# Long cross attention taken by pairs of heads, with 64-row score tiles and key copies of 16 partitions

## The reference

```
q = norm(x) @ Wq          # 128 x 256, 16 heads of 16 features
k = ctx @ Wk              # 12544 x 256
v = ctx @ Wv              # 12544 x 256
for each head h:
    s = q_h @ k_h.T / 4 + mask          # 128 x 12544
    o_h = softmax(s, axis=-1) @ v_h     # 128 x 16
x = x + concat(o) @ Wo
```

## Time and profile before

| | |
|---|---|
| median of 3 runs | 1845.32 us |
| the profiled execution | 1845.17 us |
| its span, first to last instruction | 1843.4 us |
| TensorE matmul busy | 1623.4 us (88%) |
| TensorE weight load busy | 1237.0 us (67%) |
| VectorE busy | 1068.7 us (58%) |
| ScalarE busy | 900.1 us (49%) |
| mean granted TensorE clock | 0.941 |

### The profile page before, as it was taken

One profiled execution on the slowest core, in us unless ns is written; L12 is line 12 of the kernel. 1 busy time (PEld: TensorE's weight loads), 2 busy tenths in 40 slices (PEclk: granted clock), 3 DMA queues, 4 the chain that ended last, 5 costly groups with the idle time before them and its releaser, 6 DMA issues.

```text
span 1843.4 us, 34030 instructions
## 1 busy us (share of the span) xinstructions
PE 1623.4 (88%) x13482; PEld 1237.0 (67%) x13482; DVE 1068.7 (58%) x1958; ACT 900.1 (49%) x1439; POOL 15.1 (1%) x23
## 2 busy tenths in 40 slices
PE   0597997458999999999997797999999999999499
PEld 0365476236787878888785465788878788888356
DVE  6422322447677777777785325777767777777322
ACT  0011031003777777767785120776677676778221
POOL 0000000100000000000000000000000000000000
PEclk9799988669999999999998798999999999999599
DMA  8356754127654555656332175665635446550354
GB/s 351 115 185 198 265 140 128 83 114 157 144 141 101 121 120 125 143 125 151 81 82 81 61 284 121 153 145 124 159 82 141 101 121 139 125 120 2 137 234 179
DMA packets 42811, 257.09 MB, mean 139 GB/s; under 512 B 9929, under 2 KB 10185, under 8 KB 33993
## 3 DMA queue, kind: packets, MB, share of 16 engines
q1 hardware_dynamic: 42664, 255.05, 50.0%
HBM read 152.12 MB, written 0.13 MB: 83 GB/s over the span
## 4 chain that ended last, share of the span: by engine, by line
PE 81%; DMA 7%; DVE 7%; SPq 2%; ACT 2%; issue 2%; POOL 1%; POOLq 0%; DVEq 0%; ACTq 0%
PE T L534 16%; PE O L635 12%; PE S L611 10%; PE S L539 7%; PE O L534 7%; PE T L586 6%; PE T L599 5%; PE O L697 4%; PE O L586 3%; PE O L599 3%; PE S L814 2%; DMA ctx_in<-in_ctx_cols 2%; DMA wide<-in_ctx_rows 2%; PE O L847 2%; DMA wide<-in_up_L0f 2%
## 5 line engine op out<-in xcount | busy, mean ns | idle before, releaser
L1224 DVE CUSTOM_DVE_ANT_0 sc<-S,mask_bias,small 128x896 f32<-128x896 f32 x448 | 513.3, 1146 | 181.6 <-PE S L611 180.5
L926 ACT ACTIVATE sc<-sc,small 128x1792 f32<-128x1792 f32 x224 | 399.6, 1784 | 0.0
L534 PE MATMUL T<-consts,sc 128*128 128x128 f32 (+1 forms) x2200 | 336.3, 277 | 8.8 <-ACT sc L1015 6.4
L534 PEld LDWEIGHTS T<-consts,sc 128*128 128x128 f32 (+1 forms) x2200 | 260.7, 141 | 83.4 <-issue 49.3
L912 ACT ACTIVATE pT<-T 128x512 f32<-128x512 f32 (+1 forms) x446 | 232.0, 523 | 160.3 <-PE T L534 160.3
L611 PE MATMUL S<-keys,q 128*128 128x512 f32 (+1 forms) x896 | 291.8, 407 | 1.4 <-DMA keys<-keys_hl 1.4
L635 PE MATMUL O<-pT,arena 128*32 128x128 f32 x6272 | 238.8, 276 | 0.0
L635 PEld LDWEIGHTS O<-pT,arena 128*32 128x32 f32 x6272 | 179.1, 109 | 37.4 <-issue 37.2
L534 PE MATMUL O<-consts,sc 128*128 128x128 f32 x1048 | 166.7, 276 | 0.0
L912 ACT ACTIVATE pT<-O 128x512 f32<-128x512 f32 (+1 forms) x226 | 118.0, 522 | 84.6 <-PE O L534 84.6
L534 PEld LDWEIGHTS O<-consts,sc 128*128 128x128 f32 x1048 | 125.1, 140 | 35.0 <-issue 24.2
(11 more groups left out here) (281 smaller groups left out, 1453.0 us busy)
## 6 DMA issues: line engine op xcount, KB each, us to landing
keys<-keys_hl SPq DMA_DIRECT2D x448, 224.0 KB, 5.7
ctx_in<-in_ctx_cols SPq DMA_DIRECT2D x42, 896.0 KB, 7.3
wide<-in_up_L3f SPq DMA_DIRECT2D x8, 2048.0 KB, 9.0
wide<-in_ctx_rows SPq DMA_DIRECT2D x14, 896.0 KB, 5.5
wide<-in_up_L0f SPq DMA_DIRECT2D x8, 1408.0 KB, 9.3
sc<-in_ctx_cols SPq DMA_DIRECT2D x10, 896.0 KB, 7.9
wide<-in_up_L2f SPq DMA_DIRECT2D x8, 1024.0 KB, 6.6
wide<-in_down_L2f SPq DMA_DIRECT2D x8, 1024.0 KB, 4.8
```

The lines of the kernel that those rows point to most:

```text
L534: last = nc.tensor.transpose(out[0:w, t * P:(t + 1) * P], src[:, t * w:(t + 1) * w], ident)
L926: nc.scalar.activation(sc[:, n % 3, :], sc[:, n % 3, :], ACT.Exp, bias=n_best[c % 2][:, h:h + 1], scale=-1.0, accum_out=l_new[c % 2][:, h: ...
L1224: V.tensor_tensor_reduce(sc[:, n % 3, i * HC:(i + 1) * HC], S4f[:, i * 2 * BANK:i * 2 * BANK + HC], mask_bias[:, i * HC:(i + 1) * HC], 1.0 ...
```

## The change

The heads are taken in pairs. The order of the contraction's rows changes so that each head has 64 rows of its own: head 0 of a pair rows 0 to 63, head 1 rows 64 to 127, each with four groups of 16. The queries' zeros go. A score step now makes half a chunk for both heads: for each column range one matmul on the upper 64 rows of the array and one on the lower. The turned weights of both heads (28 blocks) go in seven fillings of a bank, and `pT` holds one pair. The products of both heads are one run of 28, right behind the pair's last transposes and its second projection. Scores run one pair ahead instead of two heads. `sc` gets a fourth buffer, in unused columns of `packs`. The key copies of a half become 8 transfers, each to 16 partitions and four pairs at once (`KEY_COPIES`); for this the columns of Wk are permuted on the host. `PROJECTED` now has pairs: the first half's key pieces stand in pairs 1, 2, 2, 3 and the second's in 5, 6, 6, 7.

```diff
+PROJECTED = {0: [("V", 0), ("V", 1)], 1: [("K", 0, 0), ("V", 2)], 2: [("K", 0, 1), ("K", 0, 2)],
+             3: [("K", 0, 3), ("V", 3)], 4: [("V", 4), ("V", 5)], 5: [("K", 1, 0), ("V", 6)],
+             6: [("K", 1, 1), ("K", 1, 2)], 7: [("K", 1, 3)]}
...
-                            sp.wait_ge(s["s_ready"], 2 * (H * (c - 1) + HH * (hf + 1)))
-                        for r in range(4):
-                            for j in range(HH // 2):
-                                sp.dma_start(keys4[QR * r:QR * (r + 1), hf * HH // 2 + j, :].bitcast(F32),
-                                             keys_hl[QR * j:QR * (j + 1), r % 2, :].bitcast(F32)) \
+                            sp.wait_ge(s["s_ready"], 2 * (NP * (c - 1) + NP // 2 * (hf + 1)))
+                        for head in range(2):
+                            for r in range(4):
+                                at = HR * head + DH * r
+                                sp.dma_start(keys4[at:at + DH, hf * HH // 2:(hf + 1) * HH // 2, :].bitcast(F32),
+                                             keys_hl[HR * head:HR * (head + 1), r % 2, :].bitcast(F32)) \
                                     .then_inc(s[f"keys_in{hf}"], 16)
...
-                    for n0, n1 in ((0, BANK), (BANK, HC)):
-                        last = mm(S4f[:, half * 2 * BANK + n0:half * 2 * BANK + n1], q4[:, h, :],
-                                  keys4[:, h // 2, half * HC + n0:half * HC + n1], start=True, stop=True)
+                    for n0, n1 in ((0, BANK), (BANK, HC)):
+                        for i in range(2):
+                            own = slice(HR * i, HR * (i + 1))
+                            last = mm(S4f[:, i * 2 * BANK + n0:i * 2 * BANK + n1], q4[own, j, :],
+                                      keys4[own, j, half * HC + n0:half * HC + n1], start=True, stop=True)
...
+                    pe.wait_ge(s["t_dve"], emptied(("T", m, TURNS - 1)))
+                    pe.wait_ge(s["t_act"], emptied(("T", m, TURNS - 2)))
+                    for t in range(2 * TB):
+                        i, b = divmod(t, TB)
+                        g = t % 4
+                        at = (2 * (m % 2) + i) * P
+                        last = mm(O2[32 * g:32 * g + 32, 1, at:at + P], vv[:, c % 2, b, j * 32:(j + 1) * 32],
+                                  pT2[:, t * P:(t + 1) * P], start=(b < 4), stop=(b >= TB - 4))
...
+                for m in range(PAIRS):
+                    turn(m, 0)
+                    turn(m, 1)
+                    if m + 1 < PAIRS:
+                        scores(m + 1, 0)
+                    turn(m, 2)
+                    project(m, 0)
+                    turn(m, 3)
+                    if quad_turned(m) is not None:
+                        turn_quad(quad_turned(m))
+                    if m + 1 < PAIRS:
+                        scores(m + 1, 1)
+                    for g in range(4, TURNS):
+                        turn(m, g)
+                    project(m, 1)
+                    multiply(m)
```

ScalarE's loop over the pairs:

```diff
+                for m in range(PAIRS):
+                    if quad_turned(m) is not None:
+                        take_quad(quad_turned(m))
+                    take_turned(m, 1)
+                    take_turned(m, 2)
+                    project(m, 0)
+                    take_turned(m, 3)
+                    take_turned(m, 4)
+                    take_turned(m, 5)
+                    if m + 1 < PAIRS:
+                        soften(2 * m + 2)
+                    project(m, 1)
+                    if m + 1 < PAIRS:
+                        soften(2 * m + 3)
```

VectorE's loop over the pairs:

```diff
+                for m in range(PAIRS):
+                    c, j = divmod(m, NP)
+                    take_turned(m, 0)
+                    if m + 1 < PAIRS:
+                        for n in range(2):
+                            take_scores(2 * m + 2 + n, 0)
+                    project(m, 0)
+                    if quad_turned(m) is not None:
+                        take_quad(quad_turned(m))
+                    if m + 1 < PAIRS:
+                        take_scores(2 * m + 2, 1)
+                    take_turned(m, TURNS - 1)
+                    if m + 1 < PAIRS:
+                        take_scores(2 * m + 3, 1)
+                    project(m, 1)
```

More of the change, by code:

```diff
@@ L144, in unit_order @@
     units += [("K", 0, 1, nb) for nb in range(KEY_UNITS)]
[L145 to L150, removed]
+    for m in range(PAIRS):
+        units += [("T", m, g) for g in range(3)] + [projected(m, 0), ("T", m, 3)]
+        if quad_turned(m) is not None:
+            units.append(("O", quad_turned(m)))
+        units += [("T", m, g) for g in range(4, TURNS)] + [projected(m, 1)]
+    units.append(("O", PAIRS // 2 - 1))
+    return [u for u in units if u]
 UNITS = unit_order()
@@ L158, in emptied_by @@
 def emptied_by(u):
-    return "act" if u[0] == "T" and u[2] != 1 else "dve"
+    return "act" if u[0] == "T" and u[2] not in (0, TURNS - 1) else "dve"
 EMPTIED = {e: [0] for e in ("act", "dve")}
@@ L194, in build @@
         slots = [max(sum(PACKS[n].values()) for n in LAYERS[i::2]) for i in range(2)]
-        packs = [sb("packs0", [P, slots[0]])]
-        packs1_at = nc.sbuf_base
-        packs.append(sb("packs1", [P, slots[1]]))
+        packs = [sb(f"packs{i}", [P, slots[i]]) for i in range(2)]
+        packs1_used = max(sum(PACKS[n].values()) for n in ("L2a", "L3x", "L3f"))
+        assert packs1_used + CH <= slots[1]
         arena_at = nc.sbuf_base
@@ L1261, in cross @@
                 need(dve, "pe", f"{layer}.qT_ps")
-                def queries(ap, rows):
-                    n = rows.stop - rows.start
-                    return ap.rearrange("p (j n) -> p j n", n=P).unsqueeze(2).to_broadcast([n, NP, 2, P])
-                def own_rows(rows):
-                    n = rows.stop - rows.start
-                    return C["pair"][rows, :].unsqueeze(1).unsqueeze(3).to_broadcast([n, NP, 2, P])
-                upper, lower = slice(0, P // 2), slice(P // 2, P)
-                qT = S4f[:, 0:2 * BANK]
-                V.tensor_tensor(q4[upper].rearrange("p (j a) n -> p j a n", a=2), queries(qT[upper], upper),
-                                own_rows(upper), ALU.mult)
-                link(V.tensor_copy(q_up[lower], qT[lower]))
-                link(V.tensor_tensor(q_low[lower], qT[lower], q_up[lower].bitcast(F32), ALU.subtract))
-                done("dve", V.tensor_tensor(q4[lower].rearrange("p (j a) n -> p j a n", a=2),
-                                            queries(q_low[lower], lower), own_rows(lower), ALU.mult), f"{layer}.q4")
+                qT = S4f[:, 0:NP * P]
+                q4f = q4[:, :, :].rearrange("p j n -> p (j n)")
+                link(V.tensor_copy(q4f, qT))
+                for i in range(2):
+                    rest = slice(HR * i + 2 * DH, HR * (i + 1))
+                    last = V.tensor_tensor(q4f[rest], qT[rest], q4f[rest].bitcast(F32), ALU.subtract)
+                done("dve", last, f"{layer}.q4")
                 for b in range(VALUE_UNITS):
@@ L1608, in layout @@
     L0W = i["L0_xattn_W"]
+    turned = np.arange(D).reshape(KD, NP // 2, 2, DH).transpose(0, 2, 3, 1).ravel()
     out = {
@@ L1636, in layout @@
         "pack_L2f": pack(blocks(i["L2_ffn_gate_w"].T), *rows(i["L2_ffn_expert_bias"])),
-        "pack_L3x": pack(*[blocks(i[f"L3_xattn_W{n}"]) for n in "qkvo"]),
+        "pack_L3x": pack(blocks(i["L3_xattn_Wq"]), blocks(i["L3_xattn_Wk"][:, turned]),
+                         *[blocks(i[f"L3_xattn_W{n}"]) for n in "vo"]),
         "pack_L3a": pack(blocks(i["L3_attn_o_w"].T), *rows(i["L3_attn_q"], i["L3_attn_k"], i["L3_attn_log_decay"],
```

229 lines of the change are left out of this document (100 added, 129 removed), and 3 rows, old and new, of the table PROJECTED.

## The result

The changed kernel takes 2332.11 us (median of 4 runs, 2330.17 to 2333.79), the kernel before 1844.89 us (4 runs, 1844.13 to 1846.0): 1.264 times as long, with a 95% interval of 1.2618 to 1.2662. The forecast was 2290 us with a range of 1980 to 2400. The profiled execution of the changed kernel took 2333.8 us, its span is 2330.7.

The account below looks back on a forecast made before the run. TensorE's own work was taken to bound the kernel before. Slower key copies and waits made a layer 798 us, 221 more; twice this, 442, on 1845.2 us gave 2287, say 2290 us, range 1980 to 2400.

Parts of the forecast that it names:

- the sum: One layer, first key issue to last products: 14 x 34 + 12 x 22.5 + 9.8 + 42 = 798 us; kernel 2287.
- G: Key copy of a half chunk, issue to release: 34 us, likely ends 26 and 37, against 19.9 before.
- W: From a key copy's release to the next issue, with a wait: 2P + 0.9 = 20.5, plus 2 for clock, 22.5 us.
- what the lower clock costs: TensorE partly at 1.2 GHz instead of 2.4 behind each stop: 2 us added per release-to-issue distance.
- P: TensorE's time for a pair of heads: 9.8 us, ends 9.2 and 9.9, against 10.24 before.
- pair in the last chunk: Without projections, scores, reduction, copy, latencies and products no longer hide: 8.6 us a pair against 7.0 before.
- The signs: Key transfers at 105 to 130 GB/s, some 24 ScalarE waits over 10 us, lower clock behind stops, chunk 105 to 115 us.
- The rate: Key copies writing 16 partitions: fewer partitions, lower rate than 215 GB/s; copies slower than 24 us given 85%.
- The 64-row tiles: Score blocks of a pair, heads side by side with breaks: 1.40 us taken, ends 0.80 and 1.54, against 1.60.
- third rival: Score tiles' heads don't run side by side: pair 10.3 us, kernel 2311; inside the main case, no own chance.
- The rivals with a kept rate: 16-partition key copies keep 215 GB/s: 1871 us with breaks at 64-row tiles (9%), 1837 without (6%).
- first rival: 16-partition key copies keep 215 GB/s, with tile breaks; waits too short for the clock to fall: 1871 us, 9%.

Follow-up runs that it names:

- experiment 3: Changed kernel with wide key copies: 4 transfers a half chunk, read from all 128 partitions, written to every fourth of 128; 1816.44 us, ratio 0.9851.
- experiment 5: Kernel before, its 16 key transfers a half chunk written to every fourth of all 128 partitions instead of 32 adjacent ones; 1845.7 us, ratio 1.0007.
- 9: Kernel before, key copies in 4 transfers a half chunk, read from all 128 partitions, written to every fourth, key projection's columns reordered; 1833.12 us, ratio 0.9941.
- Experiment 2: Changed kernel, each key transfer still writing 16 partitions, but every second one of a range of 32; 1919.02 us, ratio 1.04.
- experiment 6: Kernel of experiment 3, with score matmuls of each head over all 128 rows in place of 64; 1847.91 us, ratio 1.0023.
- experiment 7: Kernel of experiment 3, a pair's value products again in two runs, with its second projection between them; 1843.94 us, ratio 1.0002.
- experiment 8: Kernel of experiment 3, last chunks' next-pair first scores and reduction ahead of this pair's first transposes and copy; 1811.69 us, repeated 1812.21 us.

## Why the prediction was right

The layer L2x took 821.9 us from the first key issue (417.52) to the end of the last products, where the sum had 798. Term by term:

| Term | Forecast | Measured |
|---|---|---|
| G, issue to release | 34 us | 34.9 in the mean of 12 steps (35.05 in the one above) |
| W, release to next issue | 22.5 | 23.15 in the mean (22.96 in the one above) |
| of W, what the lower clock costs | 2 | 2.0 |
| first issue to second | 34 + 9.8 = 43.8 | 465.63 - 417.52 = 48.1 |
| the 12 steps from second to last issue, 12 (G + W) | 678 | 697 |
| last issue to the end of the products | 34 + 42 = 76 | 77 |
| waits of ScalarE | some 24, each over 10 us | 24, 17.7 in the mean |
| P, a pair where nothing waits | 9.8 | 9.87 (experiment 3) |
| pair in the last chunk | 8.6 | 8.6 |

- **The bottleneck of before** was read rightly: TensorE. Experiments 5 and 9 show it from the other side, since copies that no longer make ScalarE wait change nothing inside the chunks.
- **The signs** came as named: 117 GB/s at a DMA share of 1.03, 24 waits of ScalarE, the lower clock behind the stops. Only the chunk's 116.1 us lie just above the 105 to 115.
- **The rate** was the step that decided. 34 us was 1 us too low; by the prediction's estimate from the Trainium skill's 109 GB/s it would be 36.5, and 117 to 122 GB/s were measured, so 35.05 lies between. The assumption that consecutive transfers overlap a little fits that, but no run tells it apart from a somewhat higher rate of the 16 partitions. That the number of partitions is what counts was wrong, as experiment 2 shows: spread over 32, 16 partitions get 210 GB/s. The number came out right all the same, with luck as far as the reason goes: the changed kernel's 16 partitions are adjacent, so few partitions and a narrow range are the same thing there. The Trainium skill, SBUF — State Buffer, Door 1: The DMA port swizzle, counts ports reached and not partitions; the traces agree at 117, 210 to 215 and 421 GB/s. The copies to every fourth of 128 stay below that last figure, at 366, and no run tells why.
- **W was nearly right, in both of its parts.** Experiment 3 gives W without a stop and without the lower clock: from the start of the key piece on ScalarE to the next issue are 594.98 - 573.83 = 21.15 us, where 2P + 0.9 = 20.5 had been taken. The 2 us added for the clock were there. The changed kernel needs 739.51 - 733.44 = 6.07 us from the release to the pair's products and experiment 3, at full clock, 578.09 - 573.83 = 4.26; from the products to the next issue both need 16.89.
```profile
739.51 1.74 PE L648 MATMUL O<-pT,arena 128*32 128x128 f32 x56
...
733.00:740.00 7.00, 5.15 (x36) 4.35 (x40) 3.89 (x7) 5.33 (x7) 0.00 (x0) 0.59 0.49 203
740.00:756.00 16.00, 16.00 (x181) 10.94 (x169) 11.06 (x21) 10.76 (x18) 0.00 (x0) 1.00 0.00 1
```
```profile
573.83 0.64 ACT L914 ACTIVATE keys_hl<-O,packs 128x448 fp32r<-128x448 f32 x1 [0.91 <-PE O L586]
...
578.09 1.74 PE L645 MATMUL O<-pT,arena 128*32 128x128 f32 x56
...
573.00:595.00 22.00, 22.00 (x223) 15.38 (x221) 17.33 (x32) 16.08 (x25) 0.00 (x0) 1.00 0.13 43
```
  Experiment 2 confirms it. Of its 24 steps, 12 have a granted clock of 1.00 in the 6 us behind the release and a W of 20.7 to 21.05; the other 12 have 0.51 to 0.72 and 22.3 to 23.0. So the lower clock costs 1.7 us behind a short stop and about 2 behind a long one, some 50 of the changed kernel's 487 us.
- **The clock cost at the start too.** From the first scores to the second issue were 465.63 - 452.38 = 13.25 us where 9.8 had been taken from before. Before, the stop ahead of it was 0.75 us, here 20.6, and the granted clock is 0.50 from 452 to 458 us. Experiment 3, at full clock there, takes 442.13 - 432.02 = 10.1.
- **The 64-row tiles** cost 0.69 a block (two of 0.40 less the 0.11 of experiment 6), two are 1.38, where 1.40 was taken. The timeline of the changed kernel has the block between two groups of transposes:
```profile
702.98 0.67 PE L617 MATMUL S<-keys,q 64*128 64x512 f32 x4
703.58 0.65 PE L631 MATMUL T<-consts,sc 128*128 128x128 f32 x4
704.07 1.89 PE L602 MATMUL O<-packs,ctx_in 128*128 128x256 f32 x8
```
  Experiment 6 shows them side by side (third rival out) and experiment 7 the merged products' 0.39 for 0.37. The Trainium skill, TensorEngine Tiling (Array Packing), Key Properties, has the drain at a change of mode; the block's 0.69 against the 0.40 of bare columns agrees with that, but does not tell it from tiles that run side by side only in part.
- **The last chunk** came out at the 8.6 us that the sequence of reductions, copy and products gave. That the number fits does not show the sequence: experiment 8 put the first scores ahead in it and gained 0.35 us a pair (2.8 / 8), not the 1.0 to 1.4 expected. Two pairs, in the changed kernel:
```profile
1197.14 1.74 PE L648 MATMUL O<-pT,arena 128*32 128x128 f32 x56 [0.83 <-DVE pT L1212]
1205.75 1.74 PE L648 MATMUL O<-pT,arena 128*32 128x128 f32 x56 [0.78 <-DVE pT L1212]
1214.40 1.74 PE L648 MATMUL O<-pT,arena 128*32 128x128 f32 x56 [0.83 <-DVE pT L1212]
```
- **The rivals with a kept rate** (1871 and 1837) are out by the 117 GB/s. With nearly before's rate, experiment 2 takes 1919 and not the first rival's 1871. The rival had G + W at 40.5 us and held the waits too short for the clock to fall. The steps there take 43.0 us in the mean ((923.37 - 450.48) / 11): G is 20.2 to 22.0, W without the lower clock 0.2 to 0.6 above the rival's 20.5, and in 12 steps of 24 the clock does fall. Over both layers the steps are 50 us longer than the rival's, the starts 5 longer and the ends 7 shorter. Without waits for keys the gain is 28 us (experiment 3), not the 80 that the prediction names.

The miss of 42 us against 2290, 45 against the 2287 of the sum, is, for L2x, 12 x 0.9 for G, 12 x 0.65 for W, 4.3 at the start and 1 at the end: 24 a layer, 48 for two.

## What to carry to other kernels

When a copy inside the chip is rearranged, look at where its destination partitions lie and how far they reach, and measure its rate with the DMA engines full; neither its bytes nor its number of partitions tells it. Look at the place read as well: experiment 5 got nothing from a wide landing alone. Compare issue-to-release with the distance to the use behind it: up to that distance a slower copy is free, beyond it each microsecond is paid at every buffer turn, three engines stop together, and TensorE's lower clock behind the stop is paid on top. A transfer that writes every n-th partition of a wide range can turn a loss into a gain without another byte saved.

## What the runs showed of the hardware that was not expected

- Copies between SBUF buffers, by where they land, with 7168-byte rows: 16 adjacent partitions 117 and 122 GB/s, every second of 32 210 GB/s, 32 adjacent 215, all with the DMA engines full. Between the first and the second (changed kernel and experiment 2) only the landing place differs.
- Every fourth of 128 gave 366 GB/s with 4 transfers that each read 128 partitions, and 216 with 16 that each read 32 adjacent ones (DMA share 0.90). Which of the two differences does it is open.
- TensorE at the lower clock (0.59 in the mean of the 7 us behind a stop of 17 us, 2.97 us for a record of 1.89) cost about 2 us of 58 on the path, although TensorE worked at it for some 4 us only (granted clock 0.50 from 734 to 737 us, 0.70 to 740). Behind a stop of 2.3 us (ahead of 605.23 in experiment 2) the clock was at 0.57 for 4 us, behind one of 2.5 us (ahead of 648.38) at 1.00.
